# Register loads bundled per engine, a place of its own for every tile's rows, and 28 products of the identity on TensorE, in a fused recurrent/expert kernel

## The reference

```
logits = x_flat @ gate_w.T
probs = softmax(logits)
topk_probs, topk_idx = top_k(probs, 2)
hidden = relu(einsum('th,ehf->tef', x_flat, w1) + b1)
all_out = einsum('tef,efh->teh', hidden, w2) + b2
y = sum(gathered(all_out, topk_idx) * topk_probs)
out = x + y
```

## Time and profile before

| | us |
|---|---|
| median of 3 runs | 519.46 (518.76 to 521.85) |
| the profiled execution, its own time | 516.84 |
| its span in the profile | 514.8 |
| busy in the span: TensorE / VectorE / ScalarE / GpSimd | 437.1 / 403.0 / 351.8 / 205.0 |
| mean granted TensorE clock, as a share of full | 0.927 |

### The profile page before, as it was taken

How to read it: one execution, slowest core, us unless ns; L and a number is a source line. 1 busy time by engine, 2 the same in 40 slices (tenths; PEclk the granted TensorE clock), 3 DMA queues, 4 the chain that set the end, 5 groups by cost and what they waited for, 6 DMA issues and landing times.

```text
span 514.8 us, 9104 instructions
## 1 busy us (share of the span) xinstructions
PE 437.1 (85%) x2391; PEld 367.1 (71%) x2391; DVE 403.0 (78%) x932; ACT 351.8 (68%) x766; POOL 205.0 (40%) x196
## 2 busy tenths in 40 slices
PE   8998999999999998999889899997019888888840
PEld 7984787777777776887767688886009787788830
DVE  2576699999999999998976999889817675667621
ACT  2335688889988888998888687985018675677710
POOL 3125343342244555230002206336600775676780
PEclk9996799999999999999989999999557998899985
DMA  3883344448544444453997112001350436676616
GB/s 101 224 217 117 140 164 163 163 173 282 218 163 169 173 187 180 188 225 123 355 361 218 46 55 84 18 28 40 110 159 1 54 72 150 130 177 173 124 18 228
DMA packets 49366, 76.85 MB, mean 149 GB/s; under 512 B 8949, under 2 KB 36278, under 8 KB 45494
## 3 DMA queue, kind: packets, MB, share of 16 engines
q1 hardware_dynamic: 36454, 59.84, 34.9%
q10 hardware_dynamic: 5232, 12.27, 6.4%
q0 software_dynamic: 7648, 4.36, 6.1%
HBM read 50.69 MB, written 18.77 MB: 135 GB/s over the span
## 4 chain that ended last, share of the span: by engine, by line
DVE 31%; PE 27%; issue 17%; DMA 14%; ACT 4%; POOL 3%; DVEq 3%; SPq 1%; ACTq 1%; POOLq 0%
DVE hid_lo L1068 10%; PE ps L1359 5%; PE ps L1360 5%; PE ps L1361 5%; DVE hid_lo L1157 4%; DVE yg L1062 4%; DMA out_d<-ysb,xrow 3%; DMA xrow<-disp 3%; DMA rawf<-in_L_ffn_w_dram 2%; DMA out_dram<-xtok 2%; PE ps L1637 2%; DVEq L1294 2%; POOL out_dram L742 2%; PE ps L1429 2%; DMA out_dram<-ysb,xrow 1%
## 5 line engine op out<-in xcount | busy, mean ns | idle before, releaser
L1068 DVE TENSOR_TENSOR hid_lo<-yg,hid_hi 128x512 fp32r<-128x512 f32 x124 | 97.2, 784 | 0.0
L797 ACT ACTIVATE hid<-ps,bias_cur 128x512 f32<-128x512 f32 x128 | 86.5, 676 | 11.4 <-PE ps L1361 10.6
L818 ACT ACTIVATE hid_hi<-yg 128x512 fp32r<-128x512 f32 x124 | 77.8, 628 | 20.5 <-DVE yg L1062 19.6
L630 POOL TENSOR_TENSOR w2l<-raw,w2h 128x128 fp32r<-128x128 f32 x32 | 25.3, 791 | 108.7 <-ACT w2h L767 108.7
L853 ACT ACTIVATE hid<-ps,cols 128x512 f32<-128x512 f32 (+3 forms) x84 | 52.8, 629 | 18.5 <-PE ps L1361 12.7
L1359 PE MATMUL ps<-in_hi,w1h 128*128 128x512 f32 x128 | 53.8, 420 | 6.3 <-POOL w1l L630 5.8
L742 POOL DMA_INDIRECT out_dram<-ysb,xrow x24 | 39.5, 1644 | 43.5 <-DVE ysb L1343 37.9
L1157 DVE TENSOR_TENSOR hid_lo<-hid,hid_hi 128x512 fp32r<-128x512 f32 (+3 forms) x84 | 50.5, 624 | 7.6 <-ACT hid_hi L857 6.5
L703 POOL DMA_INDIRECT disp<-stage,idx x32 | 34.0, 1062 | 50.3 <-issue 30.2
L1062 DVE TENSOR_TENSOR yg<-hid,h_f 128x512 f32<-128x512 f32 x60 | 50.6, 844 | 1.6 <-DMA h_f<-gt_d 1.0
L1361 PE MATMUL ps<-in_hi,w1l 128*128 128x512 f32 x128 | 51.3, 401 | 0.0
(11 more groups left out here) (232 smaller groups left out, 1209.0 us busy)
## 6 DMA issues: line engine op xcount, KB each, us to landing
gb<-gt_d SPq DMA_DIRECT2D x15, 1024.0 KB, 4.6
h_f<-gt_d SPq DMA_DIRECT2D x14, 1024.0 KB, 4.5
disp<-empty ACTq DMA_DIRECT2D x16, 616.5 KB, 6.8
w1d<-wf SPq DMA_DIRECT2D x15, 512.0 KB
rawf<-in_L_ffn_w_dram SPq DMA_DIRECT2D x16, 256.0 KB, 2.9
xrow<-disp SPq DMA_DIRECT2D x23, 137.0 KB, 2.5
raw<-in_L_ffn_We_dram SPq DMA_DIRECT2D x2, 960.0 KB, 8.4
nat<-in_x_dram SPq DMA_DIRECT2D x8, 128.0 KB, 3.1
```

Of the source, the lines that this page charges most:

```text
L797: nc.scalar.activation(hid0[:, m % 4, :], bank(4 + m % 4), ACT.Gelu, bias=bias0_cur[:, e_par:e_par + 1]).then_inc(s_hid0, 1)
L818: nc.scalar.activation(hid_hi0[:, m % 8, :], src[:, m % 4, :], ACT.Copy).then_inc(s_hi0, 1)
L1068: V.tensor_tensor(hid_lo0[:, m % 8, :], src[:, m % 4, :], hid_hi0[:, m % 8, :].bitcast(F32), ALU.subtract).then_inc(s_lo0, 1)
```

## The change

Three edits. The tables are read by `values_load_multi_w_load_instructions`, which gives all 15 values of a row of `tab` from one call: on TensorE and VectorE for the experts, on SP for the first rows and for the experts, both behind the first eight row loads. `xrow` becomes two tensors with 16 and 7 places, so that every tile has its own and its own semaphore; no load waits for scatter-adds any more, and SP issues tiles 0 to 7, the register loads, the weights of tiles 8 and 9, then all fifteen dynamic row loads in a row, then the other weights. The two tensors lie at 96 KB of each partition (where `wc2`, the second-layer weights of the masked experts, was) and at 8 KB. TensorE makes 28 products of the identity with itself between its wait for `s_b2s` and the one for `s_tab`.

```diff
-XR = 7
+XR = 16
...
-        xrow = at("xrow", 8 * KB, [P, XR, 2, ROW], F32)
+
+        xrow_a = at("xrow_a", 96 * KB, [P, XR, 2, ROW], F32)
+        xrow_b = at("xrow_b", 8 * KB, [P, NTAU - XR, 2, ROW], F32)
...
-        s_ld = [sem(f"s_ld{k}") for k in range(XR)]
+        s_ld = [sem(f"s_ld{k}") for k in range(NTAU)]
...
+        def xrow(t):
+            return xrow_a[:, t, :, :] if t < XR else xrow_b[:, t - XR, :, :]
...
-                dst = xrow[:, t % XR, :, :]
-                if t >= XR:
-                    added(sp, t - XR)
-                if t < STATIC:
-                    rows_of = disp_rs[0:TS, t, :]
-                else:
-                    first = sp.value_load(tab[0:1, 0, t - STATIC:t - STATIC + 1], min_val=0,
-                                          max_val=(RANKS - TS) * S1 + EF)
-                    rows_of = disp[bass.ds(first, TS, step=S1), :]
-                sp.dma_start(dst, rows_of.rearrange("(a p) c -> p a c", p=P)).then_inc(s_ld[t % XR], 16)
+                rows_of = disp_rs[0:TS, t, :] if t < STATIC else disp[bass.ds(first_of[t - STATIC], TS, step=S1), :]
+                sp.dma_start(xrow(t), rows_of.rearrange("(a p) c -> p a c", p=P)).then_inc(s_ld[t], 16)
...
-                e = sp.value_load(tab[0:1, 1, j:j + 1], min_val=0, max_val=EF - 1)
+                e = expert_of[j]
...
-            for t in range(XR):
+            for t in range(STATIC):
                 load(t)
             sp.wait_ge(s_tab, 2)
+            _, first_of = nc.values_load_multi_w_load_instructions(
+                tab[0:1, 0, 0:DYN], engines=[mybir.EngineType.SP], min_val=0, max_val=(RANKS - TS) * S1 + EF)
+            _, expert_of = nc.values_load_multi_w_load_instructions(
+                tab[0:1, 1, 0:DYN], engines=[mybir.EngineType.SP], min_val=0, max_val=EF - 1)
             weights(STATIC)
             weights(STATIC + 1)
-            for t in range(XR, NTAU):
+            for t in range(STATIC, NTAU):
                 load(t)
-                if STATIC + 2 <= t - 1:
-                    weights(t - 1)
-            weights(NTAU - 1)
+            for t in range(STATIC + 2, NTAU):
+                weights(t)
...
-            expert_of = [dve.value_load(tab[0:1, 1, j:j + 1], min_val=0, max_val=EF - 1) for j in range(DYN)]
+            _, expert_of = nc.values_load_multi_w_load_instructions(
+                tab[0:1, 1, 0:DYN], engines=[mybir.EngineType.DVE], min_val=0, max_val=EF - 1)
...
-                pe.wait_ge(s_ld[t % XR], 16 * (t // XR + 1))
+                pe.wait_ge(s_ld[t], 16)
...
             pe.wait_ge(s_b2s, 1)
+
+            for _ in range(28):
+                M.matmul(ps[:, 7, 0:P], ident[:], ident[:], start=True, stop=True)
             pe.wait_ge(s_tab, 2)
-            expert_of = [pe.value_load(tab[0:1, 1, j:j + 1], min_val=0, max_val=EF - 1) for j in range(DYN)]
+            _, expert_of = nc.values_load_multi_w_load_instructions(
+                tab[0:1, 1, 0:DYN], engines=[mybir.EngineType.PE], min_val=0, max_val=EF - 1)
```

More of the change, by code:

```diff
@@ L743, in _ @@
                         out=(out_rows, out2)[t % 2],
-                        out_offset=bass.IndirectOffsetOnAxis(ap=xrow[:, t % XR, a, D:D + 1].bitcast(U32), axis=0),
+                        out_offset=bass.IndirectOffsetOnAxis(ap=xrow(t)[:, a, D:D + 1].bitcast(U32), axis=0),
                         in_=ysb[:, t % 3, a, :], in_offset=None, bounds_check=NT - 1, oob_is_err=False,
@@ L901, in exps @@
                     act.wait_ge(s_g, t - 3)
-                A.activation(exf[:, t % 4, :, :], xrow[:, t % XR, :, D + 1:ROW], ACT.Exp).then_inc(s_exf, 1)
+                A.activation(exf[:, t % 4, :, :], xrow(t)[:, :, D + 1:ROW], ACT.Exp).then_inc(s_exf, 1)
             for t in range(2):
@@ L1600, in turn @@
                 for a in range(2):
-                    op = M.transpose(bank(t % 2)[:, a * P:(a + 1) * P], xrow[:, t % XR, a, 0:D], ident[:])
+                    op = M.transpose(bank(t % 2)[:, a * P:(a + 1) * P], xrow(t)[:, a, 0:D], ident[:])
                 op.then_inc(s_tr, 1)
```

## The result

The changed kernel takes 503.57 us (502.51 to 507.22), the kernel before 519.71 beside it (518.76 to 521.85, the earlier runs among them): a ratio of 0.9696, 95% interval 0.9637 to 0.9756. 16.1 us are gained; the forecast was 18.4, to 501.1, and the time lies inside the range of 495.0 to 507.0. The profiled execution took 507.22, the longest of its four, with a span of 505.5.

What follows compares the result with a forecast made beforehand. The prediction took the layer to be bound by the ring of rows and its start by VectorE's register loads; 5.8 + 13.6 - 1.0 = 18.4 us gained, so 501.1 us against the median of 519.46, range 495.0 to 507.0.

Steps and rivals of the forecast that it cites:

- the ring of rows: Layer: with seven places, row loads wait for scatter-adds four tiles behind, some 4.56 us per tile; no engine is full.
- Layer, 13.6 us: First to last scatter-add: without the wait for rows, 88.8 us against 102.4, paced by GpSimd and copies of weights.
- The rival of slow copies: Layer: with 4.8 us a copy the tile takes 4.4, 4.5 us are lost, time 505.6; chance 0.13.
- the 93 that would have made me wrong: Layer, sign of being wrong: first to last scatter-add spans over 93 us.
- the 86 to 91 that I said: Layer, expected sign: GpSimd's first to last scatter-add takes 86 to 91 us.
- Start, 5.8 us: Before tile 0's first product: VectorE's bundled load of 1.0 and fifteen checks of 4.1 us replace fifteen loads, 5.8 gained.
- One of my signs of being wrong: Start: TensorE's first product comes later than 382 us.
- Products, 0 (cost up to 2.0): Start: TensorE's 28 products end inside VectorE's cover until 379.3, cost 0; that cover gone, up to 2.0 us.
- Their benefit, 0: Start: the 28 products' clock gain is lost in the quiet before the first product; 0, bounds 0 and 3.0 gained.
- Burst of rows, -1.0: Early layer: fifteen row loads in a burst delay the first scatter-adds, between 0 and 7.5 us, 1.0 taken.
- SP: Start: SP's 30 register values take some 10 us, or 18.3 singly, hidden either way; fifteen row loads out by 400.
- The bounds of the start: Start: nothing gained if fifteen values cost fifteen loads; 8.7 us if checks go too, the rows then being late next.

Runs made afterwards that it cites:

- the variant with three places: Changed kernel with three places instead of two for the copied weights and biases, so a copy may start one tile earlier: 499.4 us, ratio 0.9596.
- the second profile: The changed kernel unaltered, run and profiled once more for a second trace: 503.54 us.
- the eight more products: Changed kernel with eight more products of the identity behind the transposes of tiles 0 and 1: 501.52 us, ratio 0.9628.

## Why the prediction was right, step by step

**Bounded by the ring of rows: right.** A place per tile alone separates 515.38 from 503.57, and no wait for rows after tile 0 is left.

**Layer, 13.6 us: 10.7 (102.37 to 91.65).** The mechanism was right, both paces too: GpSimd where nothing stops it (1.875 a step in the variant with three places, 1.89 said), copies behind it. The mis-sized term is the copy: I took 4.1 us from issue to product for all thirteen tiles, from two that had met no 16 KB fetch. Tiles 10 to 22 without a 16 KB packet in their copy had 3.4 to 4.1 us, but the two that TensorE waited for longest had 5.3 and 6.0, and the clock fell behind one. The rival of slow copies (4.8 each) had the right engine and the wrong shape: few and long, not all a little longer; nor did the waits grow to 0.3 to 0.8 every second tile, as I had said. At 91.65 the stretch was still under the 93 that would have made me wrong, and outside the 86 to 91 that I said; the second profile had 90.79, and the same layer without a fall of the clock 88.3 to 89.7, around the 88.8 of my sum.

**Start, 5.8 us: 4.4.** The load was mis-sized: 1.0 taken, 1.82 measured, 0.12 us a value. The checks were as said one by one, but with the gap of 0.39 they took 4.54 (6.36 - 1.82) and not 4.1. With both corrected my steps give 5.8 - 0.8 - 0.4 = 4.6, against 4.4; the last 0.2 is that VectorE came to its reads 11.8 us behind the ranks instead of 11.6. The second profile has 3.8 for the whole start: its reads were as long (377.43 to 383.79) but began 12.4 us behind the ranks. By the figure of about 200 ns per register in the Trainium skill, "Runtime: NRT & Kernel Launch", section "Instruction fetch mechanics", an estimate for the load is 3.0 us. The trace does not agree: its 1.82 us lie between that estimate and my 1.0.

One of my signs of being wrong was a first product later than 382. It came at 387.13. Less the 5.84 us by which the ranks ended later it came at 381.3, in the second profile at 381.9: inside, but only just, and 1.4 and 2.0 us behind the 379.9 that I had worked out.

**Products, 0 (cost up to 2.0): right.** They did hold the register load until 376.7 and the transposes to 382.89, and VectorE's reads until 386.6 hid it. **Their benefit, 0: right**, and for the reason given: the clock fell again before the first product. But I had set 0 to 3.0 without saying when it would turn; the eight more products showed 1.85 in the fill.

**Burst of rows, -1.0: not seen.** It would have shown in the first scatter-adds. GpSimd made the first twelve steps at its own pace (400.09 to 422.88, 1.90 each), and its longest wait for a landing of its own, much later, was 0.9. **SP: right.** Its fifteen loads of rows were out by 405.33, 400 said, with the earlier part 5.8 us longer; even 16.6 us of registers there were hidden.

**The bounds of the start.** That the rows are late next once the checks go was said with 8.7 us gained; measured were 8.5 (23.06 to 14.55).

**The sum.** The mechanisms held, and the sizes did not all: by the stretches the start was taken 1.4 us too large, the layer 2.9, and the burst took away 1.0 that was not lost. That the time still came within 2.5 us of the forecast owes something to the burst's term having the other sign.

## What to carry to other kernels

When a ring of buffers is opened, look for the next ring behind it (here the copies with two places), and size it by its slow members, not by two quiet ones. A bundled read of registers saves only the loads; where each value keeps its check, the checks have to be counted too. Filler products bring the clock up for the first tiles only if they last until the real work starts, and they must end before the data that it waits for is there; here that was seen in stretches of single profiles and in no median.

## What the runs showed that was not expected

- A fetch of 16,384 bytes of instructions takes 0.9 to 1.6 us on one of 16 DMA engines, and one part of a transfer under way beside it lands some 2 us late: of a copy of weights (437.25 against 435.29) or of rows (446.45 against 444.84). The share of the instruction queue in the span is 0.2%, and nothing in it points to that.
- One load of 15 registers took 1.76 to 1.82 us on TensorE and VectorE over all profiles, against 0.30 for one; a check of one value 0.275, nearly as much as its own load.
- A start at 2.4 GHz instead of 1.2 was worth 1.3 to 1.85 us of the 12.5 to 13 to the first scatter-add, less than the 3.0 that half of six busy microseconds would give.
